# Attention scores with the up-projection folded into the keys: one product per score tile, row maxima carried by DMA

## The reference

```python
c_q = h_t @ W_DQ + b_DQ                      # 32 wide
c_kv = h_t @ W_DKV + b_DKV                   # 32 wide
q = concat([c_q @ W_UQ + b_UQ, c_q @ W_QR + b_QR])   # 128 + 32, per head
k = concat([c_kv @ W_UK + b_UK, h_t @ W_KR + b_KR])  # 128 + 32, per head
attn = softmax(q @ k.T / sqrt(160))
o = attn @ (c_kv @ W_UV + b_UV)
```

## Time and profile before

| | |
|---|---|
| median of 3 runs | 1004.38 us (1001.42 to 1005.31) |
| profiled execution, its time / its span | 1002.61 us / 1000.9 us |
| busy over the span | PE 88%, DVE 71%, ACT 59%, POOL 66% |
| granted TensorE clock, mean | 0.943 |
| stage two | 86 to 605 us |

### The profile page before, as it was taken

How to read it: one execution, slowest core, us unless ns; L and a number is a source line. 1 busy time by engine, 2 the same in 40 slices (tenths; PEclk the granted TensorE clock), 3 DMA queues, 4 the chain that set the end, 5 groups by cost and what they waited for, 6 DMA issues and landing times. The chain is left out here.

```text
span 1000.9 us, 21467 instructions
## 1 busy us (share of the span) xinstructions
PE 881.8 (88%) x8406; PEld 527.7 (53%) x8406; DVE 713.9 (71%) x1315; ACT 588.0 (59%) x1004; POOL 655.7 (66%) x437
## 2 busy tenths in 40 slices
PE   4893899999999999999999988962499999999995
PEld 1350244444444444444444547862266777677764
DVE  4768888888888888888898836872075666566643
ACT  3750577777777777777777663664265446544650
POOL 4200599999999999999999993698404524442452
PEclk9995799999999999999999998985599999999998
DMA  9910000000000000000000004259525434543110
GB/s 279 339 43 0 1 2 2 2 2 2 2 2 2 2 2 2 2 2 2 2 2 1 3 1 169 99 198 320 201 69 162 143 107 140 175 142 123 43 52 19
DMA packets 48166, 71.61 MB, mean 72 GB/s; under 512 B 7508, under 2 KB 40473, under 8 KB 47938
## 3 DMA queue, kind: packets, MB, share of 16 engines
q1 hardware_dynamic: 38114, 53.13, 16.1%
q0 software_dynamic: 7680, 16.87, 5.2%
q10 hardware_dynamic: 2272, 0.24, 0.2%
HBM read 46.76 MB, written 29.67 MB: 76 GB/s over the span
## 5 line engine op out<-in xcount | busy, mean ns | idle before, releaser
L834 POOL TENSOR_TENSOR prob_lo<-prob 128x1024 f16<-128x1024 f32 x208 | 437.3, 2130 | 95.0 <-ACT prob L799 94.9
L799 ACT ACTIVATE prob<-st_ps 128x512 f32<-128x512 f32 x512 | 301.4, 597 | 131.8 <-PE st_ps L723 129.5
L859 DVE TENSOR_REDUCE part_max<-x_ps 128x1 f32<-128x512 f32 x512 | 325.1, 678 | 66.7 <-PE x_ps L733 65.7
L722 PE MATMUL st_ps<-QA,KA 128*128 128x512 f16 x512 | 198.1, 387 | 0.5 <-ACT prob L799 0.5
L723 PE MATMUL st_ps<-QB,KB 65*128 65x512 f16 x512 | 196.4, 384 | 0.0
L771 PE MATMUL acc_ps<-VV,prob 128*128 128x65 f16 x2048 | 159.3, 194 | 3.9 <-POOL prob_lo L834 3.9
L771 PEld LDWEIGHTS acc_ps<-VV,prob 128*128 128x128 bf16 x2048 | 143.6, 98 | 33.4 <-POOL prob_lo L834 6.1
L771 PE MATMUL acc_ps<-VV,prob_lo 128*128 128x65 f16 x2048 | 158.7, 194 | 0.0
L771 PEld LDWEIGHTS acc_ps<-VV,prob_lo 128*128 128x128 f16 x2048 | 134.9, 98 | 29.9
L1340 POOL DMA_INDIRECT out<-yo,xb x48 | 47.7, 993 | 153.3 <-DVE yo L1447 151.1
L732 PE MATMUL x_ps<-KA,QA 64*128 64x512 f16 x256 | 102.2, 399 | 20.8 <-DVE part_max L859 20.7
(11 more groups left out here) (177 smaller groups left out, 1346.7 us busy)
## 6 DMA issues: line engine op xcount, KB each, us to landing
w1f<-in_L_ffn_w SPq DMA_DIRECT2D x8, 1024.0 KB, 6.1
w2f<-in_L_ffn_w SPq DMA_DIRECT2D x8, 1024.0 KB, 6.1
xbuf<-zeros SPq DMA_DIRECT2D x7, 910.0 KB, 16.7
xb<-xbuf SPq DMA_DIRECT2D x8, 780.0 KB, 5.4
x<-in_L_attn_h_t SPq DMA_DIRECT2D x8, 512.0 KB, 8.9
out<-x SPq DMA_DIRECT2D x4, 1024.0 KB, 5.9
tbuf<-x SPq DMA_DIRECT2D x4, 1024.0 KB, 9.7
tbuf<-gb_row SPq DMA_DIRECT2D x4, 1024.0 KB, 4.7
```

Of the source, the lines that this page charges most:

```text
L722: mm(st_ps[i % 2][:], KA[:, at], QA[:, n % QRING, half], start=True, stop=False)
L799: nc.scalar.activation(prob[:, k, f * HALF:(f + 1) * HALF], st_ps[i % 2][:], ACT.Exp).then_inc(exp_done, 1)
L834: nc.gpsimd.tensor_tensor(prob_lo[:, k, :], prob[:, k, :], prob_top[:, k, :], ALU.subtract).then_inc(sub_pool, 1)
L859: nc.vector.tensor_reduce(part_max[:, n % 2, item // 2, item % 2:item % 2 + 1], x_ps[i % 3][:], AX.X, ALU.max).then_inc(smax_done, 1)
```

## The change

The matrix moves from the queries to the keys. Stage one no longer makes KC; it makes G the other way round, in two steps (`FOLD`), as a high part GH and a low part GL. In slots 4 and 6 `keys` replaces `query`: two products give 98 rows of key features for head p+3, ScalarE copies them to KX, and VectorE makes 33 low rows in place. A score half is one product of KX (99 rows) with CQ; a maxima item is one product of 98 rows with the same KX, of the 128 queries 8 t + j, so that the maxima come out in the order of the row, and `max_rows` with its product and its copy goes: SP sends mz itself, 8 numbers from each of 128 partitions, into row 98 of CQ. CQ gets a second copy for odd heads, made by a DMA at the start of stage two. What the engines split, the slots, the ring of three banks and the reductions stay.

```diff
@@ scores, maxima, keys on TensorE @@
-                    if k == 0:
-                        te.wait_ge(qa_done, 2 * n + f + 1)
-                        te.wait_ge(ql_done, 2 * n + f + 1)
+                    if k == 0 and f == 0:
                         te.wait_ge(mrow_in[n % 2], 16 * (n // 2 + 1))
-                    at = slice(b * S + k * P, b * S + (k + 1) * P)
-                    half = slice(f * HALF, (f + 1) * HALF)
-                    mm(st_ps[i % 2][:], KA[:, at], QA[:, n % QRING, half], start=True, stop=False)
-                    mm(st_ps[i % 2][:], KB[:, at], QB[:, n % QRING, half], start=False, stop=True).then_inc(scores_ready, 1)
-
-                def maxima(n, q):
+                    mm(st_ps[i % 2][:], KX[:, n % KRING, k * P:(k + 1) * P],
+                       CQ[:, n % 2, b * S + f * HALF:b * S + (f + 1) * HALF], start=True, stop=True).then_inc(scores_ready, 1)
+
+                def maxima(n, j, f):
                     b = n // H
-                    i = n * 16 + 2 * q
-                    if i >= 2:
-                        te.wait_ge(smax_done, i - 1)
-                    te.wait_ge(qa_done, 2 * n + q // 4 + 1)
-                    at = slice(q * P, (q + 1) * P)
-                    mm(x_ps[i % 3][:], QA[0:LR, n % QRING, at], KA[0:LR, b * S:b * S + HALF], start=True, stop=True)
-                    mm(x_ps[(i + 1) % 3][:], QA[LR:P, n % QRING, at], KC[LR:P, b, :], start=True, stop=True).then_inc(smax_ready, 1)
-
-                def side_after_query(n, f):
-
-                    if 0 <= n < HEADS:
-                        te.wait_ge(ql_done, 2 * n + f + 1)
-
-                def side_after_rows(n):
-
-                    if n >= 0:
-                        te.wait_ge(mrow_done, n + 1)
-
-                def query(n, f):
+                    i = (n * ST + j) * 2 + f
+                    if i >= 3:
+                        te.wait_ge(smax_done, i - 2)
+                    if j == 0 and f == 0:
+                        te.wait_ge(kl_done, 2 * n + 2)
+                        if n == 1:
+                            te.wait_ge(copied, 16)
+                    mm(x_ps[i % 3][:], queries_of[:, n % 2, b * P:(b + 1) * P, j],
+                       KX[0:QROWS, n % KRING, f * HALF:(f + 1) * HALF], start=True, stop=True).then_inc(smax_ready, 1)
+
+                def keys(n, f):
                     b, h = n // H, n % H
-                    if f == 0:
-                        side_after_rows(n - 2)
-                    else:
-                        side_after_query(n, 0)
-                    mm(side_ps[:], GQ[:, h, :], CQ[:, b * S + f * HALF:b * S + (f + 1) * HALF],
-                       start=True, stop=True).then_inc(q_ready, 1)
-
-                def max_rows(n):
-                    side_after_query(n + 1, 1)
-                    side_after_rows(n - 1)
-                    te.wait_ge(max_done, n + 1)
-                    mm(side_ps[0:ST, 0:P], mz[:], ident16[:], start=True, stop=True).then_inc(mrow_ready, 1)
+                    if 2 * n + f:
+                        te.wait_ge(kl_done, 2 * n + f)
+                    at = slice(b * S + f * HALF, b * S + (f + 1) * HALF)
+                    mm(side_ps[0:QROWS, :], GH[:, h, :], KA[:, at], start=True, stop=False)
+                    mm(side_ps[0:QROWS, :], GL[:, h, :], KB[:, at], start=False, stop=True).then_inc(k_ready, 1)
...
@@ VectorE @@
-                def query_low(n, f):
-                    v.wait_ge(qa_done, 2 * n + f + 1)
-                    at = slice(f * HALF, (f + 1) * HALF)
-                    nc.vector.tensor_tensor(QB[0:LR, n % QRING, at], side_ps[0:LR, :], QA[0:LR, n % QRING, at],
-                                            ALU.subtract).then_inc(ql_done, 1)
+                    v.wait_ge(smax_done, 2 * ST * (n + 1))
+                    if n >= 2:
+                        v.wait_ge(mrow_in[n % 2], 16 * (n // 2))
+                    nc.vector.tensor_reduce(mz[:, n % 2, :], part_max[:, n % 2], AX.X, ALU.max).then_inc(max_done, 1)
+
+                def keys_low(n, f):
+                    v.wait_ge(kh_done, 2 * n + f + 1)
+                    at = KX[LR:QROWS - 1, n % KRING, f * HALF:(f + 1) * HALF]
+                    nc.vector.tensor_tensor(at, side_ps[LR:QROWS - 1, :], at, ALU.subtract).then_inc(kl_done, 1)
...
@@ SyncE @@
+                sp.dma_start(CQ[0:QROWS, 1, :], CQ[0:QROWS, 0, :]).then_inc(copied, 16)
                 for n in range(HEADS):
-                    sp.wait_ge(mrow_done, n + 1)
-                    sp.dma_start(QB[LR:LR + 1, n % QRING, :].rearrange("a (t q) -> a t q", q=P),
-                                 mrow[:, n % 2, :]).then_inc(mrow_in[n % 2], 16)
+                    b = n // H
+                    sp.wait_ge(max_done, n + 1)
+                    if n >= 2:
+                        sp.wait_ge(scores_ready, 2 * ST * (n - 1))
+                    sp.dma_start(CQ[QROWS:QROWS + 1, n % 2, b * S:(b + 1) * S].rearrange("a (g t) -> a g t", t=ST),
+                                 mz[:, n % 2, :]).then_inc(mrow_in[n % 2], 16)
...
@@ stage one: ScalarE, VectorE, TensorE @@
-                    nc.scalar.activation(KC[LR:P, b, :], k_ps[LR:P, HALF:S], ACT.Identity, bias=bk[LR:P, :]).then_inc(hi_done, 1)
...
+                        i = n - FOLD
+                        heads = slice(4 * i, 4 * i + 4)
+                        nc.vector.tensor_scalar(G[:, heads, :], bank[:].rearrange("p (h c) -> p h c", h=4)[:, :, 0:QROWS],
+                                                SCALE, None, ALU.mult).then_inc(side_done, 1)
+                        v.wait_ge(side_done, n + 1)
+                        nc.vector.tensor_copy(GH[:, heads, :], G[:, heads, :]).then_inc(prep, 1)
+                        v.wait_ge(prep, i + 1)
+                        nc.vector.tensor_tensor(GL[:, heads, :], G[0:LR, heads, :], GH[0:LR, heads, :], ALU.subtract)
...
+                    elif n >= FOLD:
+                        for i in range(4):
+                            h = 4 * (n - FOLD) + i
+                            at = slice(i * P, i * P + QROWS)
+                            for r in (0, LR):
+                                mm(bank[r:r + DC, at], ukvT[:, h, 0:DC], uqT[:, h, 0:QROWS], start=True, stop=True)
+                                last = mm(bank[r + DC:r + LR, at], qr[:, h, :], ident[0:QROWS, 0:QROWS], start=True, stop=True)
```

More of the change, by code:

```diff
@@ L572, in side @@
                                                        ident[0:2 * DC, 0:2 * DC])
-                    elif n == GQS:
-                        for h in range(H):
-                            last = mm(bank[0:QROWS, h * DC:(h + 1) * DC], uqT[:, h, 0:QROWS], ukvT[:, h, 0:DC], start=True, stop=True)
+                    elif n >= FOLD:
[5 more added lines that the diff above has]
+                                last = mm(bank[r + DC:r + LR, at], qr[:, h, :], ident[0:QROWS, 0:QROWS], start=True, stop=True)
                     elif n < BIAS:
@@ L784, in _ @@
                             values(p, k)
-                        if f == 0 and is_head(nm):
-                            maxima(nm, items[0] // 2)
-                    if k in QUERY_SLOTS and is_head(p + 3):
-                        query(p + 3, QUERY_SLOTS.index(k))
+                        if is_head(p + 2):
+                            maxima(p + 2, k, f)
+                    if k in KEY_SLOTS and is_head(p + 3):
+                        keys(p + 3, KEY_SLOTS.index(k))
                     if k < ST - 1 and is_head(p):
@@ L822, in _ @@
                             exponential(n, kk, f)
-                        if f == 0 and k == ROW_SLOT and is_head(p + 1):
-                            max_rows(p + 1)
                         if f == 0 and k == ST - 1 and is_head(p):
                             out_of_psum(p)
-                    if k in QUERY_SLOTS and is_head(p + 3):
-                        query(p + 3, QUERY_SLOTS.index(k))
+                    if k in KEY_SLOTS and is_head(p + 3):
+                        keys(p + 3, KEY_SLOTS.index(k))
             @block.gpsimd
```

123 lines of the change are left out of this document (47 added, 76 removed).

## The result

| | before | after |
|---|---|---|
| median of 4 runs | 1003.13 us (1001.42 to 1005.31) | 1113.71 us (1111.98 to 1114.75) |
| ratio | | 1.1099 [1.1069, 1.113] |
| profiled execution, its time / its span | 1002.61 / 1000.9 us | 1111.98 / 1110.3 us |
| granted TensorE clock, mean | 0.943 | 0.891 |
| first and last addition of halves on VectorE | 130.8, 603.4 us | 135.1, 713.6 us |

The forecast was 1034 us in a range of 988 to 1050. The direction was right and the size wrong by 80 us, beyond the range. The last row of the table says where the time went: 4.3 us before the first finished head, 105.9 us between the first and the last (578.5 against 472.6), and 0.8 us back behind them.

The account below looks back on a forecast made before the run. TensorE bounds plain slots before; once it is relieved, VectorE is the bound. +1.1 us a head over 30 heads (+33) and -3 at stage two's start, on 1002.6, give 1032.6, as median 1034 us; range 988 to 1050.

Parts of the forecast that it names:

- A: VectorE's leg from the low part of half 0 to slot 7's first reduction: 2.89 to 2.79 us.
- B: VectorE's leg from there to slot 0's first reduction: new wait for the keys' low part, +0.58, 2.41 to 2.99 us.
- C: VectorE's leg from slot 0's first reduction to its split of tile 5: shorter TensorE slots, -0.42, 4.30 to 3.88 us.
- D: VectorE's leg from tile 5's split to the next low part: 5.56 to 6.35 us, with two splits 5.89 to 7.36.
- The order at the shared port: At tile 5's split, GpSimd's subtraction comes 0.33 us before VectorE's, which waits 1.5 us once a head.
- The rival in which VectorE still gets in first: At tile 5's split VectorE isn't blocked by GpSimd: 15.0 us a head, 989 us in total; chance 0.20.
- The clock: Rival: TensorE's clock falls as it idles some 2 us between slot 7's items and the low part; far above 1100; 0.03.
- Two key products for one query product: +0.22: Term of leg A on TensorE: one more product for the features, +0.22 us.
- no step into the half array: Term of leg A on TensorE: the change from full to half array goes away, -0.1 us.
- The start of stage two: First two turns, where only VectorE's pace counts: reductions 0.60 to 0.63 us apart instead of 0.69, -2 to -3 us.
- The strided weights: Rival: a maxima item's weight load isn't hidden, 0.1 us more each, +0.6 a head, 1052 us; chance 0.12.
- The maxima by DMA: Transfer issued after mz, needed 5.9 us later: cost from nothing to 0.3 x 32 = 10 us, taken as nothing.

Follow-up runs that it names:

- fill: Changed kernel with both TensorE idle stretches of a head filled by products nobody reads (ten and seven): 1060.77 us.
- ek_four: early_keys24 with tile 7 split on VectorE in every head, four splits of 16 instead of three: 992.05 us.
- fill_rows: fill with the second key product made over 128 rows (64 of them zero weights) instead of 64: 1048.77 us.
- start_early5: Changed kernel with tile 5's split one reduction earlier and filler products only before a head's first maxima item: 1047.87 us.
- early_keys24: Changed kernel with key features in slots 2 and 4 and both VectorE splits one reduction earlier: 975.14 us.
- ek5_rows: Changed kernel with keys in slots 2 and 4, only tile 5's split early, second key product over 128 rows, nothing filled: 964.24 us.
- keys24: Changed kernel with key features made in slots 2 and 4 instead of 4 and 6, nothing else: 1028.69 us.

## Why the forecast was too low

The head with one split, by the prediction's legs. The column `fill` is from its rows above: A is 303.86 to 306.95, B 289.89 to 293.17, C to 297.21, D to 303.86.

| leg | before | forecast | fill, clock 1.00 | after |
|---|---|---|---|---|
| A | 2.89 | 2.79 | 3.09 | 3.45 |
| B | 2.41 | 2.99 | 3.28 | 3.34 |
| C | 4.30 | 3.88 | 4.04 | 4.04 |
| D | 5.56 | 6.35 | 6.65 | 7.39 |
| head | 15.16 | 16.01 | 17.06 | 18.22 |

**What bounds the kernel, and relieving TensorE brings little.** Right. The slot of TensorE is 1.36 (forecast 1.34), and VectorE and its waits set the pace. ek_four shows the bound from the other side.

**The new wait for the keys' low part (B).** Right in its place and its mechanism: idle 0.59 for 0.6 expected.

**The order at the shared port (D).** Right: GpSimd first, by 0.37 where 0.33 was worked out, a split of 2.60 for 2.76 assumed, tile 7's untouched. The rival in which VectorE still gets in first (0.20) didn't happen.

**The clock. This is the step that failed.** "11.6 of 16.5 is nearer the first", the prediction says, and it gave the clock 0.03 and priced it as a whole stage at half clock. It had the idle time ("TensorE will idle some 2 us between its items of slot 7 and the low part") and compared means: 3.43 of 5 us busy held 1.00, 2.46 fell. But the same mean over a head can come of an even load or of full stretches with pauses of 2 us between them, and here it was the second. In the trace the fall comes head by head, for some 3 us, at or behind the end of such a pause. `fill` prices it: 1113.7 - 1060.8 = 53 us. Nor was the second pause in the forecast: the blocked split was charged to VectorE, and that TensorE stands behind it for 1.7 us was not followed up. The Trainium skill, TensorE: Matmul & The Clock Gate, HAM oscillation, tells of a kernel whose TensorE waits between its tiles and meets the low clock anew each time. The trace agrees in kind, though its pauses are shorter than the page's: 0.91 in heads with one fall, 0.83 in heads with two, 1.00 with the pauses filled.

**Terms that were too small, 27 us.** `fill` against the forecast is 17.06 for 16.0 and 17.77 for 17.0 a head: 0.9 on average. That 30 x 0.9 is 27 too is chance, since the trace has 28 whole heads with maxima, not the 30 that the forecast counted. By the additions of halves, `fill` has 56.3 us more than before between the first and the last, for 33 forecast, so 23 too many; the start has 2.8 for -3, so 6 too many; and 1.5 come back behind the last.
- *The key products.* "Two key products for one query product: +0.22" left out that the second works on 64 rows. The prediction took 0.1 off leg A for "no step into the half array" and had the price from the earlier trace rows, but did not see that the change brings the same step in twice a head. fill_rows: 0.47 and 0.24 a head, 0.36 on average, or 10 us in 28 heads, and 2.8 us at the start.
- *Hand-offs on VectorE.* The addition of halves follows a single reduction by 0.72 (310.18 to 310.90) where 0.61 stood (145.65 to 146.26), the low part follows mz by 0.20 where 0.08 stood, the split of tile 5 follows the start of slot 2's two reductions by 1.32 (two slots of 1.36 behind 313.52, so 316.24, to 317.56) where 1.21 stood (151.15 to 152.36), and the low part of half 0 follows the start of slot 5's by 1.33 (`fill`) where 1.20 stood. So 0.1 each in several places, spread over all legs; in C it is most of the 0.16. No row of before told this. The traces do hold a pattern. Before, all of VectorE's instructions in stage two start at partition 0; in the change the low part of the keys reads and writes from partition 64 on (rows LR to QROWS - 2). In the changed kernel, fill, start_early5, early_keys24 and ek5_rows the distance is the long one (0.71 or 0.72 for 0.60, 0.20 for 0.09 behind mz) at the low part itself, at a reduction right behind it (0.72 for 0.60), and at the first instruction behind it that reads SBUF, which is the addition or tile 5's split. Tile 7's split, which has tile 5's between it and the low part, keeps 0.60. These are five places a head of 0.11 or 0.12, or 0.56 us, and 0.55 is what `fill_rows` leaves above the forecast (17.06 on average for 16.5). No run made the low part at partition 0, so this cause is read off the traces and not tested.
- *The start of stage two.* Forecast -3, measured +4.3. The reductions do come 0.60 apart instead of 0.69, as forecast, but TensorE has the key products at half clock between them, and from 100 us to the first addition the mean clock is 0.71 where it was 0.77. With fillers it is +2.8, and with 128 rows too 0.0 (130.78 us). This was small but of the wrong sign.

Together: 1034 + 53 + 27 = 1114. The start missed by 7.3 us in all, of which 1.5 are in the clock's part and the rest in the second.

**The strided weights (rival, 0.12).** Not seen. The load is longer, but each product still follows at 0.22, so that the load is hidden. The Trainium skill, SBUF, Specifications, speaks of lines of 16 bytes and a penalty for a reader that crosses to a new one each time; the load bears this out in kind (147 ns for 111), and the products don't pay for it:

```profile
L726 PEld LDWEIGHTS x_ps<-KX,CQ 98*128 98x128 f16 x512 | 75.1, 147 | 198.7 <-issue 97.3
...
L714 PEld LDWEIGHTS st_ps<-CQ,KX 99*128 99x128 f16 x512 | 56.5, 111 | 32.6 <-issue 14.8
```

**The maxima by DMA.** No wait of TensorE for mrow_in stands among the waits of the changed kernel. The nothing that was taken holds.

## What to carry to other kernels

An engine that is relieved starts to pause, and for TensorE a pause has a second price: look at where each pause is and how long, not at the busy share of a stretch. If a pause can't be removed, products that nobody reads are a cheap test of what the clock costs. A change that is right on the engine's list may need the neighbours' lists rearranged before it pays: here the same products were 11% slower, and with two moves and a full-height product 3.8% faster. When two engines share a port, work out who arrives first to a tenth of a microsecond after every change, at each meeting, since a fix at one meeting can make the next.

## What the runs showed of the hardware

- TensorE's clock fell to 1.2 GHz for some 3 us behind a pause of 1.7 us between full stretches (the starts around it are 318.76 and 320.82, the fall in 322.0 to 322.5), while a pause of 2.3 us (before 313.07) passed without one. In start_early5 it fell at 282.1 behind two pauses of 0.8 and 0.9 us, 0.4 us apart. Which of them is followed by a fall wasn't settled by these runs.
- A product over 64 rows between products over 128 costs 0.1 us on either side, with 98 columns of weights (0.31, 0.35) and with 128 (0.32, 0.32). 98 columns of weights instead of 128 cost 0.03.
- Where the start partition changes between 0 and 64 on VectorE (the five places of a head named above), an instruction follows at 0.71 or 0.72 us instead of 0.60: it starts 0.03 behind the end of the one before (310.90 behind 310.18 + 0.69) where others start 0.08 ahead of it (146.26). No run isolates it.
- In a meeting at the shared port the one behind waits for the rest of the other's instruction. VectorE's 1.39 in ek5_rows ends at 280.40, 1.08 us after GpSimd's split (275.58 + 3.74 = 279.32); 1.60 (GpSimd's ends at 274.06), 2.09 in start_early5, 2.46 in keys24 and 2.60 in the changed kernel give the same 1.08. Both can pay: GpSimd's instruction right behind takes 1.59 for 0.61 (274.02). Behind 279.32 GpSimd had nothing to do for 0.94 us and paid nothing.
